# Attention phases rebuilt: scores as 32-row products per head, weighted sums as 64x64 products, dense products dealt out between small steps

## What is computed

```python
q = (x @ Wq.T).reshape(B, N, 12, 32); k = ...; v = (x @ Wv.T + bv)...      # layer 0
a = einsum('bnhd,bmhd->bhnm', q, k) * 384**-0.5 + adj[:, None]
a = where(all(a == 0, -1), -inf, a);  a = nan_to_num(softmax(a))
return einsum('bhnm,bmhd->bnhd', a, v).reshape(B, N, 384) @ Wo.T + bo

q = split_heads(x @ Wq + bq); k = ...; v = ...                            # layer 3
s = einsum('bhqd,bhkd->bhqk', q, k) / sqrt(32) + beta * adj
s = where(adj > 0, s, -9e15)
return merge_heads(einsum('bhqk,bhkd->bhqd', softmax(s), v))
```

## Time and profile before

| what | value |
|---|---|
| median of 3 runs | 3057.83 us (3057.32 to 3061.69) |
| the profiled execution itself | 3053.92 us |
| its span | 3052.2 us |
| mean granted clock of TensorE | 0.983 |
| PE, PEld busy | 2759.9 us (90%), 2344.4 us (77%) |
| DVE, ACT, POOL busy | 1828.1 (60%), 1302.7 (43%), 1098.5 us (36%) |

### The profile page before, as it was taken

The page is one execution under the profiler, slowest core; times in us unless marked ns, Lnnn a source line. Parts: engine busy times, 40 slices in busy tenths (PEclk is TensorE's granted clock), DMA queues, the critical chain, the costliest instruction groups (busy, mean ns, idle before and its releaser), DMA issues. The chain is left out here.

```text
span 3052.2 us, 62873 instructions
## 1 busy us (share of the span) xinstructions
PE 2759.9 (90%) x23168; PEld 2344.4 (77%) x23168; DVE 1828.1 (60%) x4275; ACT 1302.7 (43%) x2260; POOL 1098.5 (36%) x1103
## 2 busy tenths in 40 slices
PE   6888888886899999999968999999999968888888
PEld 5777777775688888888858888888888857777676
DVE  5766766765454555545545787878787744444454
ACT  3434434433444444444433343434343345555554
POOL 2333323333233223322332444444444433444443
PEclk9999999999899999999988999999999989999999
DMA  4111111112321122112121111111111122222221
GB/s 136 58 52 55 58 50 60 55 48 70 103 64 40 52 72 72 31 52 73 47 73 43 47 57 46 58 45 57 46 57 37 44 79 65 65 65 65 66 77 53
DMA packets 185095, 182.73 MB, mean 60 GB/s; under 512 B 78032, under 2 KB 184528, under 8 KB 185040
## 3 DMA queue, kind: packets, MB, share of 16 engines
q1 hardware_dynamic: 185040, 181.98, 19.2%
HBM read 131.61 MB, written 50.33 MB: 60 GB/s over the span
## 5 line engine op out<-in xcount | busy, mean ns | idle before, releaser
L52 PE MATMUL l_psW<-w_hi,l_hT_hi 128*128 128x384 f32 x1920 | 681.3, 355 | 46.3 <-DVE l_vX L508 26.4
L52 PE MATMUL l_psW<-w_hi,l_hT_lo 128*128 128x384 f32 x1920 | 647.3, 337 | 0.0
L52 PE MATMUL l_psW<-w_lo,l_hT_hi 128*128 128x384 f32 x1920 | 645.0, 336 | 0.0
L52 PEld LDWEIGHTS l_psW<-w_hi,l_hT_hi 128*128 128x128 f32 x1920 | 361.7, 188 | 101.5 <-DVE l_vX L508 37.9
L52 PE MATMUL l_psW<-l_hT_hi,w_hi 128*128 128x512 f32 x1008 | 408.9, 406 | 11.0 <-ACT l_m L1042 4.0
L52 PE MATMUL l_psW<-l_hT_hi,w_lo 128*128 128x512 f32 x1008 | 396.3, 393 | 0.0
L52 PE MATMUL l_psW<-l_hT_lo,w_hi 128*128 128x512 f32 x1008 | 395.9, 393 | 0.0
L52 PEld LDWEIGHTS l_psW<-w_lo,l_hT_hi 128*128 128x128 f32 x1920 | 362.5, 189 | 1.3
L52 PEld LDWEIGHTS l_psW<-w_hi,l_hT_lo 128*128 128x128 f32 x1920 | 361.6, 188 | 0.0
L275 POOL TENSOR_TENSOR l_s_d<-l_s_b,l_mx 128x768 f32<-128x768 f32 x128 | 188.5, 1472 | 359.1 <-DVE l_mx L494 359.1
L1042 ACT ACTIVATE l_m<-l_psW 128x512 f32<-128x512 f32 x192 | 114.7, 598 | 324.0 <-PE l_psW L52 324.0
(11 more groups left out here) (178 smaller groups left out, 5429.6 us busy)
## 6 DMA issues: line engine op xcount, KB each, us to landing
after_l<-l_xr SPq DMA_DIRECT2D x192, 192.0 KB, 1.9
l_xr<-after_l SPq DMA_DIRECT2D x48, 768.0 KB, 4.5
l_xl<-after_l SPq DMA_DIRECT2D x47, 768.0 KB, 5.0
l_xl<-in_x SPq DMA_DIRECT2D x16, 768.0 KB, 4.9
l_xr<-in_x SPq DMA_DIRECT2D x16, 768.0 KB, 4.5
out_x<-l_xr SPq DMA_DIRECT2D x64, 192.0 KB, 2.9
l_adj<-in_adj SPq DMA_DIRECT2D x48, 128.0 KB, 2.3
l_adj<-in_adj SPq DMA_DIRECT2D x128, 32.0 KB, 2.1
```

What stands on the lines that cost most here:

```text
L52: last = nc.tensor.matmul(out, lhs[a](c), rhs[b](c), start=(m == 0), stop=(m == n - 1))
```

## The change

The two attention phases are written anew; l1, l2, the arithmetic of the layers and the weights' use are as before.

- `scores`: one product per head and graph, 32 rows of q (stationary, 64 columns) against 64 columns of k: 24 products for each tile in place of 12, each in a tile of 32 rows by 64 columns of the array. The keys are stored once (`kT`), and the masks, the second ACTIVATE and `by_halves` (the order of columns of Wq and Wk) are gone. The four heads of a chunk write to four banks of `psS`.
- `weigh`: one product per head and graph with 64 rows (the keys of a graph) and 33 columns, 24 for each tile in place of 12, into the free columns of the four `psS` banks. `vX` has no zeros.
- In l0 the copies of queries move from DVE to ACT. `transposes` go through `psP`, `out_transposes` through `psW`. `psT` and `psO` are gone.
- `s_b`, `mx`, `mn`, `vX`, `oT_hi`, `oT_lo` hold four tiles in place of one or two.
- The order of every engine is rewritten. On PE a dense block stands between nearly all small steps: queries, keys and values of the next group are dealt out over the turn, and in l0 two of the four `project` blocks of a group are done in the next turn. Scores of the next group's tile 0 end the turn. Statistics and normalising run two groups ahead.
- On SP the residual rows `xr` are reloaded tile by tile behind each store. The loops are written as a first turn, a loop of 13, and two last turns.

Cut to its core (the new order of ACT and POOL, and the end of the old one of PE, are left out):

```diff
-    kX = sb("kX", [P, KC, 2 * TILES, 2, NODES])
-    k_mask = sb("k_mask", [P, 2])
-    b_kX = None if proj else sb("b_kX", [P, 2, KC])
-    s_b = sb("s_b", [P, 2, HEADS, NODES])
+    kT = sb("kT", [P, KC, COLS])
+    s_b = sb("s_b", [P, TILES, HEADS, NODES])
     s_d = sb("s_d", [P, HEADS, NODES])
...
+    vX = sb("vX", [P, TILES, 2, PAIRS, HD + 1])
     o_rows = sb("o_rows", [P, 2, D])
...
+    last = GROUPS - 1
+    q_bank, k_bank, v_bank = ((0, 1, 1), (0, 0, 0), (1, 0, 1, 1)) if proj else ((0, 0, 0), (1, 1, 1), (0, 1, 0, 1))
...
+    def turns(engine, turn):
+
+        turn(0, True, True, True)
+        with engine.Fori(1, last - 1) as i:
+            turn(i, False, True, True)
+        turn(last - 1, False, True, False)
+        turn(last, False, False, False)
...
+        def queries(i, c):
+            act.wait_ge(q_done, i * KC + c + 1)
+            nc.scalar.activation(qT[:, c, :], psW[q_bank[c]][:], ACT.Copy, scale=scale).then_inc(q_set, 1)
...
+            if proj:
+                nc.scalar.activation(kT[:, c, :], psW[k_bank[c]][:], ACT.Copy).then_inc(k_set, 1)
...
+        def projected_turn(i, opening, ahead, further):
+            step.turn(i, before if ahead else before - 2)
+            add_bias(i, 1)
+            if ahead:
+                hT_parts(i + 1, 0)
+                hT_parts(i + 1, 1)
+            maximum(i, 1)
+            add_bias(i, 2)
+            values(i, 3)
+            least(i, 1)
+            row_output(i, 0)
             if ahead:
                 hT_parts(i + 1, 2)
                 hT_parts(i + 1, 3)
-                if not proj:
-                    score_bias(i + 1)
-            row_output(i, TILES - 1)
-            if ahead:
+            add_bias(i, 3)
+            maximum(i, 2)
+            oT_parts(i, 0)
+            maximum(i, 3)
+            least(i, 2)
+            if further:
+                statistics(i + 2)
+            if ahead:
+                values(i + 1, 0)
+            row_output(i, 1)
+            oT_parts(i, 1)
+            if further:
+                shifts(i + 2)
+            least(i, 3)
+            row_output(i, 2)
+            if ahead:
+                values(i + 1, 1)
+            oT_parts(i, 2)
+            row_output(i, 3)
+            if ahead:
+                values(i + 1, 2)
+                add_bias(i + 1, 0)
+                maximum(i + 1, 0)
+            oT_parts(i, 3)
+            if ahead:
+                least(i + 1, 0)
+
...
         def scores(i, t):
-            if t == 0:
-                pe.wait_ge(q_set, i * KC + KC)
-                pe.wait_ge(hT_set, i * TILES + TILES)
-            else:
-                wait_apart(s_read, i * TILES + t)
             for c in range(KC):
-                if t == 0:
-                    wait_apart(k_set, i * KC + c + 1)
-                for b in range(2):
-                    rows_b = slice(NODES * b, NODES * (b + 1))
+                for r in range(HPC):
+                    head = slice(HD * r, HD * (r + 1))
                     for g in range(2):
-                        lo = t * P + g * NODES
-                        ins = nc.tensor.matmul(psS[NODES * g:NODES * (g + 1), b, c * P:(c + 1) * P],
-                                               qT[rows_b, c, lo:lo + NODES],
-                                               kX[rows_b, c, 2 * t + g].rearrange("p h n -> p (h n)"),
-                                               start=True, stop=True)
+                        nodes = slice(t * P + g * NODES, t * P + (g + 1) * NODES)
+                        ins = nc.tensor.matmul(psS[NODES * g:NODES * (g + 1), r, c * NODES:(c + 1) * NODES],
+                                               qT[head, c, nodes], kT[head, c, nodes], start=True, stop=True)
             ins.then_inc(s_done, 1)
...
-                pe.wait_ge(o_set, i * TILES + t)
+            wait_apart(v_set, i * TILES + t + 1)
+            wait_apart(eT_set, i * TILES + t + 1)
             for a in range(PAIRS):
-                for g in range(2):
-                    ins = nc.tensor.matmul(psO[NODES * g:NODES * (g + 1), a * 2 * (HD + 1):(a + 1) * 2 * (HD + 1)],
-                                           eT[:, a, NODES * g:NODES * (g + 1)],
-                                           vX[:, t % 2, g, a].rearrange("p b d -> p (b d)"), start=True, stop=True)
+                for b in range(2):
+                    c, r = divmod(2 * a + b, HPC)
+                    keys_b = slice(NODES * b, NODES * (b + 1))
+                    for g in range(2):
+                        ins = nc.tensor.matmul(psS[NODES * g:NODES * (g + 1), r, S_end + c * (HD + 1):S_end + (c + 1) * (HD + 1)],
+                                               eT[keys_b, a, NODES * g:NODES * (g + 1)], vX[keys_b, t, g, a],
+                                               start=True, stop=True)
             ins.then_inc(o_done, 1)
...
+        def project(i, t, bank, transposed=None):
+            pe.wait_ge(oT_set, i * TILES + (t + 1 if transposed is None else transposed))
+            oT = tuple((lambda c, x=x: x[:, t, c, :]) for x in (oT_hi, oT_lo))
+            split_matmul(nc, psW[bank][:, 0:D], oT, w_cols(O, slice(0, D))).then_inc(y_done, 1)
+
+        def projected_turn(i, opening, ahead, further):
+            n = i + 1
+            wait_apart(s_read, i * TILES + 1)
+            scores(i, 1)
+            if ahead:
+                pe.wait_ge(hT_set if opening else eT_set, i * TILES + (TILES if opening else 0))
+                transposes(n, 0)
+                transposes(n, 1)
+            if not opening:
+                project(i - 1, 2, 0, transposed=TILES)
+            wait_apart(s_read, i * TILES + 2)
+            scores(i, 2)
+            pe.wait_ge(hT_set if ahead else eT_set, n * TILES + 2 if ahead else i * TILES)
+            exp_transposes(i, 0)
+            pe.wait_ge(v_set if opening else y_read, i * TILES + (3 if opening else -2))
+            values(i, 3)
+            wait_apart(s_read, i * TILES + 3)
+            weigh(i, 0)
+            if ahead:
+                pe.wait_ge(eT_set, i * TILES + 1)
+                transposes(n, 2)
+                transposes(n, 3)
+            if not opening:
+                pe.wait_ge(y_read, i * TILES - 1)
+                project(i - 1, 3, 0)
+            wait_apart(o_set, i * TILES + 1)
+            scores(i, 3)
+            pe.wait_ge(v_set, i * TILES + 4)
+            out_transposes(i, 0)
+            if ahead:
+                if not opening:
+                    pe.wait_ge(y_read, i * TILES)
+                pe.wait_ge(hT_set, n * TILES + TILES)
+                queries(n, 0)
+            else:
+                pe.wait_ge(eT_set, i * TILES + 1)
+            exp_transposes(i, 1)
+            if ahead:
+                pe.wait_ge(oT_set, i * TILES + 1)
+                values(n, 0)
+            wait_apart(s_read, i * TILES + 4)
+            weigh(i, 1)
+            if ahead:
+                pe.wait_ge(q_set, n * KC + 1)
+                keys(n, 0)
+                pe.wait_ge(v_set, n * TILES + 1)
+            else:
+                pe.wait_ge(oT_set, i * TILES + 1)
+            out_transposes(i, 1)
+            pe.wait_ge(eT_set, i * TILES + 2)
+            exp_transposes(i, 2)
+            if ahead:
+                pe.wait_ge(k_set, n * KC + 1)
+            else:
+                pe.wait_ge(y_read, i * TILES)
+            project(i, 0, 0)
+            if ahead:
+                pe.wait_ge(oT_set, i * TILES + 2)
+                queries(n, 1)
+            wait_apart(o_set, i * TILES + 2)
+            weigh(i, 2)
+            if ahead:
+                pe.wait_ge(y_read, i * TILES + 1)
+                values(n, 1)
+                pe.wait_ge(q_set, n * KC + 2)
+            else:
+                pe.wait_ge(oT_set, i * TILES + 2)
+            out_transposes(i, 2)
+            pe.wait_ge(eT_set, i * TILES + 3)
+            exp_transposes(i, 3)
+            if ahead:
+                pe.wait_ge(v_set, n * TILES + 2)
+                keys(n, 1)
+                pe.wait_ge(oT_set, i * TILES + 3)
+                queries(n, 2)
+            wait_apart(o_set, i * TILES + 3)
+            weigh(i, 3)
+            if ahead:
+                pe.wait_ge(k_set, n * KC + 2)
+                keys(n, 2)
+                pe.wait_ge(q_set, n * KC + 3)
+                values(n, 2)
+                wait_apart(o_set, i * TILES + 4)
+                wait_apart(k_set, n * KC + 3)
+                scores(n, 0)
+            else:
+                pe.wait_ge(y_read, i * TILES + 1)
+            out_transposes(i, 3)
+            if ahead:
+                pe.wait_ge(v_set, n * TILES + 3)
+            project(i, 1, 1)
+            if not ahead:
+                project(i, 2, 0, transposed=TILES)
+                pe.wait_ge(y_read, i * TILES + 2)
+                project(i, 3, 1)
+
...
+            wait_apart(s_read, i * TILES + 1)
+            scores(i, 1)
+            if ahead:
```

(70 more changed lines are left out.)

610 lines of the change are left out of this document (311 added, 299 removed).

## The result

The changed kernel takes 2988.93 us (median of 4 runs, 2986.17 to 2989.18), the kernel before, measured beside it, 3059.57 (3057.32 to 3061.69): ratio 0.9767, 95% interval [0.975, 0.9784]. That is 71 us less. It is faster, as forecast, and inside the range, but 130 us less were forecast: a little over half of it came.

A forecast was written before the change was run, and what follows sets the result against it. PE was taken as the bound, the fullest engine in both attention phases. Savings of 35 us in l0 and 95 in l3, together 130, gave 2928 us against a median of 3057.8; the range was 2855 to 3010.

The forecast's parts named there:

- PE's work is paid at the full granted clock: Both attention phases: PE durations were taken at granted clock 1.00, its upper level of 2.4 GHz.
- DVE paces l0's turn up to the output of tile 1: l0: DVE sets PE's out_transposes(1) at 25.3 us, then PE runs 17.7; a turn is 43.0 us, 2.2 less.
- ACT paces l3's start, queries 0 wait: l3: queries 0 wait until 11.6 us, PE idle 2.8, then 18.6 of work; a turn is 30.2 us, 6.1 less.
- Scores at 0.34 a tile: Scores on PE: 48 rows in groups of eight take 0.34 us, 0.3 less per tile, 1.2 us a turn.
- the dear end: Scores on PE: if only four products run together, a tile's scores take 0.67 us, no gain.
- Weighed sums at 0.69: Weigh on PE: queued weight loads set 0.69 us a tile against 0.73 before, counted as no gain.
- Copies, masks, SP's waits at nothing: Copies on ACT and DVE, the masks' setup and SP's added waits for `stored` cost nothing; SP at most one landing per turn.
- Ends: Outside the repeated turns: l0 +4 at first scores, -4 in its last turn (32 us); l3 +1.6 and -4.5.
- The price of a start (27 ns): Rival, chance 0.12: scores and weigh are paid by product starts, 27 and 30 ns a row; 3027 us.
- My 1.2 us: Scores or weigh: time of a block of 48 product rows at the Trainium skill's 25 ns from start to start.
- The strips in series: Rival, chance 0.06: scores' 32-row strips do not run side by side, 2.8 us a tile; 3108 us.
- The queues wait where I see no wait: Rival, chance 0.12: unseen waits between engine queues cost 2.5 us a turn in both phases, 75 us; 3003 us.

The follow-up runs named there:

- e1: The changed kernel with unread filler products on PE, nine before l0's output transposes of tile 1 and seven before l3's queries 0: 2958.72 us.
- e3: e2 plus, in l3, ACT making the high parts of the next group's tiles 2 and 3 before the exponentials of tile 1: 3025.42 us.
- e8: The changed kernel with only SP's load of xl in l0 issued one group further ahead, order otherwise the same: 2984.13 us, measured once.
- e2: The changed kernel with DVE's statistics in l0 moved earlier, behind the add of tile 2: 3054.12 us.
- e9: e5 with the projects of tiles 1 and 2 in l0's last turn moved to where PE waits: 2918.6 us.
- e10: e5 with 12, 9 and 7 unread filler products before the output transposes of tiles 1, 2 and 3 in l0's last turn: 2919.69 us.
- e5: e3 with SP's load of xl in l0 issued one group further ahead, between the stores of tiles 0 and 1: 2921.41 us.
- e7: e1 with every scores product issued twice into the same places, 96 product rows a block in place of 48: 3007.18 us, measured once.

## Why the prediction was right in its sign and half right in its size

The step that failed first is the unspoken one under all durations: that PE's work is paid at the full granted clock. I read 1.00 in the earlier trace rows, where PE's idle time lay in many stops of up to 1.25 us, and gathered the new order's idle time into one stop of 2 us (l0) and 1.25 (l3) without asking what the clock does behind it. It fell in 21 of 30 turns and cost 1.6 us each time. What the 65 us that are missing in the span are made of:

| item | us | from |
|---|---|---|
| clock behind the stop, 11 turns of l0 and 10 of l3 | +33 | 44.02 against 42.45, 33.55 against 31.93; e1 gives 30.2 |
| l3's turn at full clock, 31.95 for 30.2 | +26 | 15 x 1.75 |
| l0's turns at full clock | -12 | 47 less over 15 turns, 35 forecast |
| ends of l0 | +13 | +5.5 and +7.2, forecast +4 and -4 |
| ends of l3, and l1 and l2 | +6 | +2.7, forecast -3 |

Point by point:

- *DVE paces l0's turn up to the output of tile 1.* Right: the transposes come 24.45 us into the turn (343.85 to 368.30), 25.3 forecast; from there to the next scores a full-clock turn needs 18.0, 17.7 forecast. 42.45 against 43.0.
- *ACT paces l3's start, queries 0 wait.* The mechanism is right (e3 takes it away and gets 31.04), the size is off: queries 0 come at 12.73 (2631.47 to 2644.20) instead of 11.6, and what follows takes 19.2 instead of 18.6, because a 512-column block behind a small step takes 2.13 to 2.26 us to the next block, not the 2.05 of two dense blocks in a row. Before queries 0 PE's own work was undersized: 11.2 us (12.73 less the stops of 1.25 and 0.29), not 8.8. A scores block takes 0.71 to the next block, where my sum had 0.34 for its products, and a 384-column block behind it 1.76 or 1.77, not 1.6. So the product of values 3 is late, ACT waits 0.79 for it (row above), and its high parts end at 11.9 us, not 11.05; DVE's low parts add the rest. By the trace that fits the 1.1 us; no run took them apart.
- *Scores at 0.34 a tile.* The last product row starts 0.57 into the block; taken was 0.34, the dear end was 0.67. The strips do run side by side, but the pace of 7 ns holds only for the beginning. *Weighed sums at 0.69*: 0.90 less the length of one row, 0.69. Right.
- *Copies, masks, SP's waits at nothing.* Right for this order (e8: 5 us at most). e2 shows the cover was thin: with the statistics 10 us earlier it costs some 5 us a turn.
- *Ends.* The last turn of l0 was taken as 32; it is 43.75, at a mean clock of 0.83. With e9's order and e10's clock, on e5, it comes to 37.4 and 39.3: the DVE path that I counted is not alone there, small steps wait for each other and three projects stand behind the last output.
- *The rivals.* The price of a start (27 ns) is out: 12 ns on average, and 10 for each of 48 more (e7). The Trainium skill (TensorE: Matmul & The Clock Gate, Part 1) puts the floor from start to start near 25 ns. My 1.2 us took a row for a product; a block has 24 products, so by that page it would be 0.6 us, an estimate that lies near the 0.57 measured. Still the rows do not bear the floor out for products on different tiles: it is 14 ns a product for the first four and 20 for each of the 24 more in e7. In its section Why this matters for your kernels the Trainium skill says that products on different row groups start within 4 ns of each other; here the first rows are 7 ns apart, the nearest to it. The strips in series are out too (0.71 us a block, not 2.8). "The queues wait where I see no wait" came nearest in time, 3003, but not in kind: the 1.6 us a turn are no wait, they are PE at its lower level. Where waits go (e5) the time is 2921, near the forecast's 2928, by another way.

## What to carry to other kernels

When an order gathers PE's idle time in one place, read the granted clock behind that place before pricing the work there: here a stop of 1.3 to 2 us cost 1.6 us more behind it in 21 of 30 turns, about as much as itself. The length of the stop does not tell beforehand: the kernel before stood as long as 1.25 us and kept its clock. Either cut the stop or spread it; a filler shows in one run what it costs. And a step that is moved earlier needs its data earlier: look first at when the queue issues the load.
